# A cross-attention and mixture-of-experts layer on one core: token rows laid out by partition in HBM, two sums moved to GpSimd, and the first rows sent in another order

## The reference

```python
# attention, 16 heads of 16 channels, causal
qp = layernorm(x) @ Wq.T
k, v = split(ctx @ Wkv_expand.T, 2)
attn = softmax(where(causal, (qh @ kh.T) / sqrt(16), min))
x = x + (attn @ vh) @ Wout.T
# mixture of experts on the T = 1024 tokens, E = 16 experts, the best 4 of each token
h = layernorm(x)
w, i = top_k(softmax(h @ gate_w.T), 4);  w = w / w.sum()
# each expert takes its first CAP = 128 tokens, in the order of the tokens
for e in range(16):
    eout[e] = (silu(xg[e] @ w_gate[e]) * (xg[e] @ w_up[e])) @ w_down[e] * w_of_slot[e]
y = scatter_add(eout)
x = x + y + silu(h @ sw_gate) * (h @ sw_up) @ sw_down
```

## Time and profile before

| | us |
|---|---|
| median of 3 runs | 202.97 |
| the three runs | 202.97, 204.8, 201.26 |
| the profiled execution | 200.8 |
| its span, first to last instruction | 199.1 |
| PE busy in the span | 180.5 (91%) |
| DVE busy | 125.7 (63%) |
| POOL busy | 97.1 (49%) |
| ACT busy | 80.2 (40%) |
| mean granted clock of TensorE | 0.993 of full |

### The profile page before, as it was taken

The page is one execution under the profiler, slowest core; times in us unless marked ns, Lnnn a source line. Parts: engine busy times, 40 slices in busy tenths (PEclk is TensorE's granted clock), DMA queues, the critical chain, the costliest instruction groups (busy, mean ns, idle before and its releaser), DMA issues.

```text
span 199.1 us, 3911 instructions
## 1 busy us (share of the span) xinstructions
PE 180.5 (91%) x1364; PEld 136.4 (69%) x1364; DVE 125.7 (63%) x360; ACT 80.2 (40%) x173; POOL 97.1 (49%) x129
## 2 busy tenths in 40 slices
PE   7989799899887999899989897998999999999990
PEld 2666676586654876569747685787877888777870
DVE  2794686977599259964494646888676554353054
ACT  2584456573286227550468313512133333332000
POOL 7836791868783004620055000043687888777202
PEclk9999999999999999999999999999999999999997
DMA  5856665111598368411951075954145444545786
GB/s 173 219 146 203 183 192 154 43 44 55 154 333 256 95 183 264 136 53 34 287 177 57 0 240 174 311 161 161 56 79 79 57 91 93 79 59 72 174 278 211
DMA packets 22459, 28.94 MB, mean 145 GB/s; under 512 B 2457, under 2 KB 17801, under 8 KB 22441
## 3 DMA queue, kind: packets, MB, share of 16 engines
q1 hardware_dynamic: 18944, 23.06, 38.3%
q0 software_dynamic: 3184, 5.38, 13.8%
q10 hardware_dynamic: 313, 0.27, 0.4%
HBM read 15.91 MB, written 6.42 MB: 112 GB/s over the span
## 4 chain that ended last, share of the span: by engine, by line
PE 56%; DVE 7%; issue 2%; ACT 1%; DVEq 1%; ACTq 0%
PE s_ps L1608 10%; PE s_ps L1502 9%; PE m_ps L1627 7%; PE m_ps L1518 6%; PE m_ps L1578 5%; PE m_ps L1460 3%; PE o_ps L1422 3%; PE t_ps L1596 2%; PE o_ps L1618 2%; DVE top L932 2%; PE t_ps L1540 2%; PE m_ps L1484 2%; PE t_ps L1406 2%; PE m_ps L1437 1%; PE m_ps L1472 1%
## 5 line engine op out<-in xcount | busy, mean ns | idle before, releaser
L565 POOL TENSOR_SCALAR_AFFINE_SELECT probs<-probs 128x256 f32<-128x256 f32 (+1 forms) x48 | 23.0, 486 | 42.5 <-ACT probs L708 41.5
L932 DVE TENSOR_REDUCE top<-s_ps 128x2 f32<-128x512 f32 (+1 forms) x48 | 32.1, 685 | 8.2 <-PE s_ps L1372 7.6
L708 ACT ACTIVATE probs<-t_ps 128x512 f32<-128x512 f32 x48 | 27.6, 597 | 8.8 <-PE t_ps L1406 6.0
L1502 PE MATMUL s_ps<-xn_t,sgu 128*128 128x256 f32 (+1 forms) x96 | 23.5, 384 | 0.7 <-DVE s_mid L1017 0.7
L1406 PE MATMUL t_ps<-q_rows,k_rows 128*128 128x256 bf16 (+1 forms) x128 | 19.6, 247 | 1.9 <-ACT probs L708 1.1
L1502 PEld LDWEIGHTS s_ps<-xn_t,sgu 128*128 128x128 f32 (+1 forms) x96 | 16.5, 182 | 3.9 <-DVE s_mid L1017 1.1
L1369 PE MATMUL s_ps<-mask_b,ident_b 128*128 128x256 bf16 (+1 forms) x48 | 14.9, 311 | 3.9 <-DVE top L932 3.3
L1372 PE MATMUL s_ps<-k_rows,q_rows 128*128 128x128 bf16 (+1 forms) x128 | 18.3, 246 | 0.0
L630 POOL DMA_INDIRECT xn<-xn_d,tok_i x4 | 3.9, 978 | 23.9 <-DVE tok_i L1110 23.3
L1136 DVE TENSOR_TENSOR e_mid<-s_ps,e_act 128x176 f32<-128x176 f32 x16 | 5.5, 341 | 14.5 <-ACT e_act L756 13.3
L1406 PEld LDWEIGHTS t_ps<-q_rows,k_rows 128*128 128x128 bf16 x128 | 10.1, 98 | 6.4 <-ACT probs L708 2.9
(11 more groups left out here) (191 smaller groups left out, 387.7 us busy)
## 6 DMA issues: line engine op xcount, KB each, us to landing
k_rows<-k_parts SPq DMA_DIRECT2D x24, 128.0 KB, 2.4
q_rows<-q_parts SPq DMA_DIRECT2D x24, 128.0 KB, 2.4
k_rows<-in_w_dn SPq DMA_DIRECT2D x12, 176.0 KB
out<-xs SPq DMA_DIRECT2D x8, 256.0 KB, 2.3
wgu_early<-in_w_gu SPq DMA_DIRECT2D x4, 352.0 KB
q_rows<-in_w_gu SPq DMA_DIRECT2D x4, 352.0 KB
v_ones<-in_w_gu SPq DMA_DIRECT2D x4, 352.0 KB
probs<-in_w_gu SPq DMA_DIRECT2D x4, 352.0 KB
```

The source lines that it names most:

```text
L565: nc.gpsimd.affine_select(out=v, in_=v, compare_op=ALU.is_ge, fill=0.0, base=0, pattern=[[0, v.shape[1]], [1, P]], channel_multiplier=-1). ...
L708: t_ring.emptied(nc.scalar.activation(probs[:, g % 2, u, :], t_ring.bank(job)[:], ACT.Exp, scale=HD ** -0.5), job)
L932: s_ring.emptied(nc.vector.tensor_reduce(dst, src, AX.X, ALU.max), job)
L1502: last = nc.tensor.matmul(s_ring.bank(("gu", b, c))[0:size, S * half:S * half + S], sgu[:, hc, half, at:at + size], xn2_t[:, hc, S * b:S * ...
```

## The change

It has three parts.

**The rows in HBM.** In `out`, `xn2_d` and `odd_d` the token at partition p of tile t now stands in row p*8 + t (`by_token`, and the rearrangement `(p t)` for the zeros of `odd_d`), where it stood in row t*128 + p. What a partition holds of a batch is one run of 2 KB, and what it holds of four tiles one run of 4 KB. The constants of the row numbers change with it, at the same instructions. The host puts the rows of the result back in order. The rows that one expert gathers and scatters are the same tokens in the same order, but inside a tile neighbours are a multiple of 8 KB apart, where it was a multiple of 1 KB.

**The end.** The semaphores of the loads become two, one for each half of the tiles, which both accumulators raise. POOL adds the second accumulator for batch 2 and batch 3, one behind the other. DVE first adds it for the batches 0 and 1, and then adds the four PSUM banks in order.

**The opening.** SP sends all 6 DMAs of the keys of batch 0 before those of the queries, and the 4 unread products ahead of `("s", 0, 0)` are gone.

```diff
-KEEP_BUSY = {("k", 0): 11, ("q", 0): 3, ("x", 1): 2, ("s", 0, 0): 4}
+KEEP_BUSY = {("k", 0): 11, ("q", 0): 3, ("x", 1): 2}
...
+        def by_token(d):
+
+            return d[0:T].rearrange("(p t) c -> p t c", t=NT)
...
-                rows_of("k", b, 0)
-                if b == 0:
-                    rows_of("q", b, 0)
-                rows_of("k", b, 1)
-                rows_of("k", b, 2)
-                for part in range(1 if b == 0 else 0, 3):
-                    rows_of("q", b, part)
+                for k in "kq":
+                    for part in range(3):
+                        rows_of(k, b, part)
...
-            for n, (acc, dst, done) in enumerate(((out, xs, out_in), (odd_d, odd_rows, odd_in))):
+            for n, (acc, dst) in enumerate(((out, xs), (odd_d, odd_rows))):
                 sp.wait_ge(scattered[n], 16 * ((E - LATE) // 2))
                 for i in range(2):
-                    rows, tiles = slice(T // 2 * i, T // 2 * i + T // 2), slice(NT // 2 * i, NT // 2 * i + NT // 2)
-                    sp.dma_start(dst[:, tiles], acc[rows].rearrange("(t p) c -> p t c", p=P)).then_inc(done[i], 16)
+                    tiles = slice(NT // 2 * i, NT // 2 * i + NT // 2)
+                    sp.dma_start(dst[:, tiles], by_token(acc)[:, tiles]).then_inc(sums_in[i], 16)
...
-                        pool.dma_start(odd_d.rearrange("(t p) c -> p t c", p=P),
+                        pool.dma_start(odd_d.rearrange("(p t) c -> p t c", p=P),
...
-            v = slice(QT * (B - 1), QT * B)
-            pool.wait_ge(out_in[1], 16)
-            pool.wait_ge(odd_in[1], 16)
-            nc.gpsimd.tensor_tensor(xs[:, v], xs[:, v], odd_rows[:, v], ALU.add).then_inc(odd_added, 1)
+
+            pool.wait_ge(sums_in[1], 32)
+            for b in range(B // 2, B):
+                v = slice(QT * b, QT * b + QT)
+                nc.gpsimd.tensor_tensor(xs[:, v], xs[:, v], odd_rows[:, v], ALU.add).then_inc(pool_added, 1)
+                pool.wait_ge(pool_added, b - B // 2 + 1)
...
-            chained(add_sum(0))
-            link(add_sum(1))
-            add_odd(0).then_inc(result_ready, 1)
-            add_odd(1).then_inc(result_ready, 1)
-            link(add_sum(2))
-            add_odd(2).then_inc(result_ready, 1)
-
-            dve.wait_ge(odd_added, 1)
-            add_sum(3).then_inc(result_ready, 1)
+            for b in range(B // 2):
+                add_odd(b)
+            dve.wait_ge(dve_chain, n_chain[0])
+            for b in range(B):
+                result(b)
```

More of the change, by code:

```diff
@@ L369, in build @@
         spread_ready = sem("spread_ready")
-        out_in = [sem(f"out_in{i}") for i in range(2)]
-        odd_in = [sem(f"odd_in{i}") for i in range(2)]
-        odd_added = sem("odd_added")
+        sums_in = [sem(f"sums_in{i}") for i in range(2)]
+        pool_added = sem("pool_added")
         result_ready = sem("result_ready")
@@ L420, in send_rows @@
                     after_shift(b - ROW_BUFS + 1)
[L421 to L427 removed]
+                for k in "kq":
+                    for part in range(3):
+                        rows_of(k, b, part)
             def store_base(b):
                 m_ring.wait_emptied(sp, ("shared" if b < B - 1 else "wo", b))
[L432 removed]
+                sp.dma_start(by_token(out)[:, QT * b:QT * b + QT],
                              xs[:, QT * b:QT * b + QT]).then_inc(acc_stored, 16)
@@ L449, in store_normalised @@
                 sp.wait_ge(xn2_ready, QT * (b + 1))
-                sp.dma_start(xn2_d[S * b:S * b + S].rearrange("(t p) c -> p t c", p=P),
+                sp.dma_start(by_token(xn2_d)[:, QT * b:QT * b + QT],
                              xn2[:, b % 2]).then_inc(xn2_stored[b % 2], 16)
@@ L586, in late_constants @@
                                     allow_small_or_imprecise_dtypes=True))
-                link(nc.gpsimd.iota(minus_slot[:], pattern=[[0, 1]], base=0, channel_multiplier=-1,
+                link(nc.gpsimd.iota(minus_slot[:], pattern=[[0, 1]], base=-T, channel_multiplier=-1,
                                     allow_small_or_imprecise_dtypes=True))
-                link(nc.gpsimd.iota(cst[:], pattern=[[0, P]], base=0, channel_multiplier=1,
+                link(nc.gpsimd.iota(cst[:], pattern=[[0, P]], base=0, channel_multiplier=NT,
                                     allow_small_or_imprecise_dtypes=True))
@@ L592, in late_constants @@
                 link(nc.gpsimd.tensor_copy(tok_vals[:, :, :, 0], v))
-                link(nc.gpsimd.iota(v, pattern=[[P, NT], [0, E]], base=-T, channel_multiplier=0,
+                link(nc.gpsimd.iota(v, pattern=[[1, NT], [0, E]], base=0, channel_multiplier=0,
                                     allow_small_or_imprecise_dtypes=True))
@@ L616, in _ @@
                         pool.wait_ge(shift_in[1], 16)
-                        pool.dma_start(odd_d.rearrange("(t p) c -> p t c", p=P),
+                        pool.dma_start(odd_d.rearrange("(p t) c -> p t c", p=P),
                                        zero_rows[:].unsqueeze(1).to_broadcast([P, (T + CAP) // P, H])).then_inc(zeros_stored, 16)
                     if (b, g) == (2, 1):
-                        constant(nc.gpsimd.iota(token_iota, pattern=[[1, T]], base=0, channel_multiplier=0,
+                        constant(nc.gpsimd.iota(token_iota.rearrange("p (t n) -> p t n", t=NT), pattern=[[1, NT], [NT, P]], base=0, channel_multiplier=0,
                                                 allow_small_or_imprecise_dtypes=True))
@@ L1157, in add_odd, with result @@
                 v = slice(QT * b, QT * b + QT)
-                dve.wait_ge(odd_in[b // 2], 16)
-                return nc.vector.tensor_tensor(xs[:, v], xs[:, v], odd_rows[:, v], ALU.add)
-            def add_sum(b):
+                dve.wait_ge(sums_in[b // 2], 32)
+                chained(nc.vector.tensor_tensor(xs[:, v], xs[:, v], odd_rows[:, v], ALU.add))
+            def result(b):
                 job, ring = SUMS[b], sum_rings[b]
                 ring.wait(dve, job)
-                dve.wait_ge(out_in[b // 2], 16)
+                if b >= B // 2:
+                    dve.wait_ge(pool_added, b - B // 2 + 1)
                 v = xs[:, QT * b:QT * b + QT]
-                return nc.vector.tensor_tensor(v, ring.bank(job)[:].rearrange("p (t c) -> p t c", t=QT), v, ALU.add)
+                nc.vector.tensor_tensor(v, ring.bank(job)[:].rearrange("p (t c) -> p t c", t=QT), v,
+                                        ALU.add).then_inc(result_ready, 1)
             def stats_of(b):
@@ L1678 @@
     r = run_bass_kernel_spmd(nc, [arrays], core_ids=[0])
-    return r.results[0]["out_0"][0:T].reshape(B, S, H)
+    return lay(r.results[0]["out_0"][0:T].reshape(P, NT, H), 1, 0, 2).reshape(B, S, H)
```

3 lines of the change are left out of this document (1 added, 2 removed).

## The result

The changed kernel took 205.12 us (median of 4 runs, 204.46 to 206.88), the kernel before 202.12 us in the same session (4 runs, 200.94 to 204.8). The ratio is 1.0184, 95% interval 1.0138 to 1.0229: slower, by 2.8 to 4.6 us; whether by more than 2% these runs don't settle. The forecast was 201.5 in a range of 199.2 to 204.0, so the sign and the range were both wrong. The profiled execution after took 204.46 with a span of 202.7, against a span of 199.1 before.

A forecast was written before the change was run, and what follows sets the result against it. PE was taken to bound nearly all the middle, leaving gains only at both ends: opening -1.3, second POOL addition +0.9, loads -0.5, with the last store -1.0 rounded, from 202.5 to 201.5 us; range 199.2 to 204.0.

The forecast's parts named there:

- The opening: Start of the scores: query rows in by 16.9, PE ready at 17.10, first score 1.34 us earlier than 18.44; taken as -1.3.
- The two adders: At the end: POOL's two additions in series, 2 x 1.27 us, then DVE's last of 0.68; +0.9 us on the path.
- The collision: At the end: DVE's second addition still running when POOL wants to start; taken as 0, with +0.5 kept in the range.
- I take -0.5: Four accumulator loads at the end, 2.1 MB in 4 KB instead of 1 KB runs: 0.5 us sooner.
- the rule of the Trainium skill: DMA line rate is reached from 512 B runs up, so longer loads gain 0; as a rival 202.1 us, chance 0.15.
- The stores ... of the base rows, now in 2 KB runs, lie under PE's work: Stores of `xn2_d` and the base rows, hidden under PE's work, were put at nothing.
- The clock: TensorE's clock at the opening: the removed products leave a gap of 0 to 0.6 us, so no clock effect.
- Scatters land later: Rival at the end: 8 KB row pitch slows each scatter; 0.6 us each gives 203.3 us; chance 0.14.
- The opening's gain is taken back in the middle by a wait tied to something I overlooked: Rival: the opening's 1.3 us is lost again before the end, giving 202.5 + 0.9 - 0.5 = 202.9 us; chance 0.12.
- three signs of being wrong: Middle not moving by 1.3 us; scatter distance changing from 4.6 us; POOL's first addition over 6.2 us behind odd loads' issue.
- The third: Sign of being wrong at the end: POOL starts its first addition later than 6.2 us behind the odd loads' issue.

The follow-up runs named there:

- Short or late stores: Changed kernel, base stores of batches 2 and 3 in 1 KB runs (ratio 1.0058 to before), or issued only after the first four gathers landed (1.0086).
- short loads: Changed kernel with the loads of `out` as four DMAs of every second tile, in 1 KB runs: 203.21 us, ratio 1.0103 to the kernel before.

## Why the prediction was wrong

**The opening: right.** The order of the DMAs ran as worked out, twelve in 7.7 us (forecast 12 x 0.63 = 7.6), and PE had no wait for the rows. The first score came at 17.10 where the first load was in time, and at 17.71 where it was not. Over the 14 traces with the new opening it came at 16.89 to 18.35, median 17.35. The old opening had 18.44 and 18.36, besides 20.73 in the one execution with the slow start. So about 1.1 us is the usual gain. The forecast of -1.3 stands against -0.8 in the profiled execution, and -1.0 and -1.6 us by the two ratios of the opening alone. That the gain lasts to the experts was right as well.

**The two adders: right.** Landing to the end of DVE's last addition was forecast as 2.54 + 0.1 + 0.68 = 3.3 us and came as 3.40 (196.50 to 199.90), where it was 2.42. POOL's additions took 1.27 each, back to back. The collision did not come. DVE's two additions of the second accumulator were done as POOL began (195.22 + 1.29 = 196.51), so both kept their normal duration, and none showed the 1165 ns of the earlier trace rows. The cost repeats: from POOL's first addition to the end of the span it is 5.1 to 5.5 us in the five traces with the old end and 5.9 to 6.3 in the twelve with the new one.

**"I take -0.5" for the loads: wrong.** The term priced the loads by themselves. By themselves it holds, 8.48 against 8.89 us. But their first half runs beside the last scatter, and the stretch that counts, scatter to POOL, went from 10.31 to 11.40, +1.1. I had the scatter's 4.09 us in the rows, and had the loads' first issue ahead of its landing in the same rows, and added them as if neither touched the other. No trace with the new rows has an end stretch under 11.39 us, where the term asked for 9.8; so the gain failed to come. That it came as a loss of 1.1 us rests on the first measurements alone. By the rule of the Trainium skill that I had set against the term ("DMA: Bandwidth & Descriptors", Specifications) it would have been 0. That is nearer to +1.1 than -0.5 is, but the rule gives no loss either, and the loads alone took 8.48 and 8.89 us, not the same.

**"The stores ... of the base rows, now in 2 KB runs, lie under PE's work": wrong.** SP's two stores do lie under PE's work, but the gather of expert 1 doesn't. It took 4.9 us with the stores beside it, and had 3.5 at most before. PE waited 0.36 us for it, and then came a stretch of half clock: together +2.2 us by the account. Short or late stores gave 1.0 to 1.3% back. This was the largest single item, and the forecast had it at nothing because it asked what the stores wait for, not what shares the engines with them.

**The clock: put at nothing for the wrong place.** I looked at the gap that the 4 unread products leave, and no low stretch came there. It came at 139.5 us, after PE had stood still 0.57 us, as before, and then 0.36 us more. The forecast had no term for a clock loss behind a lengthened wait.

**The rivals.** "Scatters land later" had the right sign, and the last scatter did land 1.8 us later. Its mechanism was wrong in both halves: alone a scatter is hardly slower for the 8 KB steps (3.91 against 3.77 us), and the delay does not repeat. The change's last three scatters into `odd_d` start 4.51 and 4.84 us apart (175.75, 180.26, 185.10), as before. "The opening's gain is taken back in the middle by a wait tied to something I overlooked" is in effect what happened at 137 us, at 2.2 us where the rival had priced it at 1.3. Its chance of 0.12 and the 0.14 of the other were stated as alternatives, while both came true together. That is also how the range failed: its upper end took one loss at a time. And of the three signs of being wrong that the forecast named, only the first showed (the middle moved by 0.8, not 1.3 us). The third, POOL over 6.2 us behind the issue of the odd loads, read 5.48, because it counted from an issue that had itself moved.

## What is settled and what is open

Shown: the new rows are the whole loss. About half of it or more goes with the base stores' long runs beside the gathers: with them there, four traces of four have a late gather and a low clock behind it, and taking them away, by time or by length, brings 1.0 to 1.3% back. The scatter by itself and the loads by themselves are not slower beyond 0.14 us, in one trace each.

Not shown: that the new rows lengthen the end stretch. In the first measurements it was 1 us longer with them, in the later ones the two overlap.

Open: why scatter and loads overlapped less well in most traces with the new rows. A late landing of the scatter that leaves the engines half empty is seen in the changed kernel, and short loads remove it without a gain. The place of the rows in HBM is what is left over, but nothing here measures it by itself, and with ratios of 1.0039 and 1.0005 in one session the residue is not certain to be more than noise. Open too: what brings the clock down in a given run. A wait of PE stands in front of it in the changed kernel, but not in the one with late stores, nor in the one with the new end alone.

## What to carry to other kernels

A DMA is not free because nobody waits for it. Before you put a transfer at nothing, list what else is on the DMA engines from its issue to its landing, and ask of each whether someone waits for that; a gather in small pieces that PE needs next is the first to look for. Measure an end made of several transfers from the start of the first to the landing of the last, since speeding one of them may only move the wait to the next. Trace the same kernel twice before you read 1 us out of a single pair. Where two losses have different places, let the range hold both at once.

## What the hardware showed that I had not expected

- The half clock costs more than the wait in front of it: 0.53 us of shift up to the transposes of expert 1, then 1.71 us by the next mark, 6 us later, with PE busy throughout.
- A gather of 1 KB pieces took 4.8 to 5.1 us at most beside stores in 2 KB runs, and 3.0 to 4.2 us in all other traces.
- From its start to the issue of the next load, a scatter of 1 KB pieces took 3.8 to 3.9 us alone, 4.1 to 6.3 beside loads in 1 KB pieces, and 5.9 to 7.0 beside loads in 4 KB pieces. The total of scatter and loads didn't follow (11.39 against 11.40 us).
- Pieces of 4 KB gave the same 2.1 MB only 0.4 us sooner than pieces of 1 KB in the old rows (8.48 against 8.89), each traced once.
